# GNN layer, one core: a new order of work at the entry to the joint loop, and of the marks in the last three steps

## What is computed

```python
h = jnp.maximum(_layernorm(x, axis=-1), 0.0)
rel_inputs    = concatenate([h[senders], h[receivers], relations], axis=-1)
rel_effects   = relu(rel_inputs @ re_w1 + re_b1) @ re_w2 + re_b2
agg_effects   = segment_sum(rel_effects, receivers, num_segments=50000)
effect_inputs = concatenate([h, agg_effects], axis=-1)
out = x + relu(effect_inputs @ ea_w1 + ea_b1) @ ea_w2 + ea_b2
```

## Time and profile before

| | |
|---|---|
| median of 3 runs | 955.74 us (954.33 to 956.46) |
| the profiled execution, its own time | 956.01 us |
| its span | 954.1 us |
| PE busy | 923.3 us, 97% of the span |
| PE weight loads | 817.8 us, 86% |
| DVE busy | 740.1 us, 78% |
| ACT busy | 605.5 us, 63% |
| POOL busy | 609.1 us, 64% |

### The profile page before, as it was taken

The page is one execution under the profiler, slowest core; times in us unless marked ns, Lnnn a source line. Parts: engine busy times, 40 slices in busy tenths (PEclk is TensorE's granted clock), DMA queues, the critical chain, the costliest instruction groups (busy, mean ns, idle before and its releaser), DMA issues.

```text
span 954.1 us, 21049 instructions
## 1 busy us (share of the span) xinstructions
PE 923.3 (97%) x6450; PEld 817.8 (86%) x6450; DVE 740.1 (78%) x2155; ACT 605.5 (63%) x1180; POOL 609.1 (64%) x600
## 2 busy tenths in 40 slices
PE   4879999999999999999999999999999999999987
PEld 4668998898898899889889889988988988998876
DVE  5887788788788878878877887886887788788562
ACT  1447666666666766666666676666666667666653
POOL 7785776776677677677667767767766776772320
PEclk7979999999999999999999999999999999999999
DMA  6253655555565565555556556555555655554442
GB/s 200 75 148 113 183 163 168 150 177 175 151 186 168 151 183 163 168 151 176 172 155 185 167 153 183 162 169 158 169 174 151 186 167 152 169 177 146 124 123 76
DMA packets 114105, 151.88 MB, mean 159 GB/s; under 512 B 17984, under 2 KB 70080, under 8 KB 113984
## 3 DMA queue, kind: packets, MB, share of 16 engines
q1 hardware_dynamic: 101440, 124.73, 43.2%
q0 software_dynamic: 12544, 25.72, 10.2%
HBM read 104.92 MB, written 45.46 MB: 158 GB/s over the span
## 4 chain that ended last, share of the span: by engine, by line
PE 94%; DVE 3%; SPq 1%; issue 1%; ACT 1%; DMA 0%; DVEq 0%
PE l_ps L531 33%; PE l_ps L546 27%; PE l_ps L536 17%; PE agg_ps L496 7%; PE edge_ps L479 4%; PE node_ps L487 4%; PE node_ps L471 1%; SPq L294 0%; DVE rel_row L831 0%; DVE hot L844 0%; SPq L300 0%; DVE lo L804 0%; DVE h L797 0%; DMA drow_i<-in_dst_rows 0%; DMA win<-rel_rows 0%
## 5 line engine op out<-in xcount | busy, mean ns | idle before, releaser
L386 POOL DMA_INDIRECT gath<-in_x,dst_all x196 | 200.2, 1022 | 59.7 <-issue 59.7
L386 POOL DMA_INDIRECT gath<-in_x,src_all x196 | 195.0, 995 | 52.9 <-issue 51.7
L546 PE MATMUL l_ps<-w2n,hid 128*128 128x128 f32 x1568 | 193.6, 277 | 0.0
L655 ACT ACTIVATE hid<-l_ps,b1n 128x512 f32<-128x512 f32 x196 | 135.0, 689 | 82.4 <-PE l_ps L536 82.4
L409 POOL TENSOR_TENSOR ea_lo<-ea_in,ea_hi 128x512 fp32r<-128x512 f32 x45 | 74.3, 1651 | 171.6 <-ACT ea_hi L629 171.6
L546 PEld LDWEIGHTS l_ps<-w2n,hid 128*128 128x128 f32 x1568 | 182.9, 192 | 0.1
L810 DVE SCALAR_TENSOR_TENSOR lo<-node_ps,hi 128x512 fp32r<-128x512 f32 x98 | 67.3, 687 | 146.1 <-ACT hi L638 146.1
L663 ACT ACTIVATE h<-xin,shift,rs 128x128 f32<-128x128 f32 x392 | 165.2, 486 | 0.0
L531 PE MATMUL l_ps<-hi,w1n_hi 128*128 128x512 f32 x392 | 155.7, 397 | 0.4 <-ACT hid L655 0.4
L531 PE MATMUL l_ps<-hi,w1n_lo 128*128 128x512 f32 x392 | 155.4, 396 | 0.0
L402 POOL TENSOR_TENSOR xb<-xin,b2n 128x512 f32<-128x512 f32 x98 | 131.0, 1354 | 33.5 <-DVE res L838 33.5
(11 more groups left out here) (98 smaller groups left out, 1566.1 us busy)
## 6 DMA issues: line engine op xcount, KB each, us to landing
win<-rel_rows SPq DMA_DIRECT2D x392, 98.0 KB
xin<-in_x_tiles SPq DMA_DIRECT2D x98, 256.0 KB, 4.2
out<-res SPq DMA_DIRECT2D x98, 256.0 KB, 3.4
rel_rows<-rel_row SPq DMA_DIRECT2D x49, 392.0 KB, 2.4
ea_in<-in_ea_t SPq DMA_DIRECT2D x49, 256.0 KB, 3.2
gath<-in_x,src_all POOLq DMA_INDIRECT x196, 2.7
gath<-in_x,dst_all POOLq DMA_INDIRECT x196, 2.9
w1e<-in_L_gnn_re_w SPq DMA_DIRECT2D x1, 384.0 KB, 3.6
```

What stands on the lines that cost most here:

```text
L386: nc.gpsimd.indirect_dma_start(gath[b][:, s, k, :], None, x, bass.IndirectOffsetOnAxis(ap=idx[:, e * T + k:e * T + k + 1], axis=0)).then_i ...
L546: last = nc.tensor.matmul(l2_ps[turn % 2][:, k * P:(k + 1) * P], hid[r][:, c, k * P:(k + 1) * P], w[:, c, :], start=(c == 0), stop=(c == C ...
L655: nc.scalar.activation(hid[r][:, c, :], l1_ps[c][:, :], ACT.Relu, bias=b[:, c:c + 1]).then_inc(hid_set, 1)
```

## The change

On POOL the copies of the destinations of groups 0 and 1 (`set_dst`) go behind the gathers of group 1 instead of one in each step, that of group 2 behind the gathers of group 4, and the first pair's two `keep_x` move from ahead of group 5's gathers to behind the lo part of group 4's edge features. For the first, DVE makes the float copy of the destinations (`dst_f`) right behind `compare_rows`.

On ACT the first pair's two `normalise` move from the end of edge step 2 to either side of its first `hidden`. On PE only the transposes of tile 1 of the first pair stay ahead of joint step 3; its sum, and tile 2's transposes and sum, go behind the first layer of edge group 3. ACT and DVE follow: in joint step 3 the first pair's sums are split after the edges' `hidden` on ACT and, on DVE, after the statistics of group 4 and pair 1.

In the three pair steps DVE does `mark` of the next tile 1 ahead of `prepare`, and `mark` of the next tile 2 ahead of tile 1's lo parts. Nothing else in the pair steps is changed, on no engine.

```diff
@@ POOL
+            set_dst(0)
+            set_dst(1)
             def edge_step(e, last, fast):
-                set_dst(e)
                 if e + 2 < EG:
                     gather(e + 2)
-                if last:
+                if e > 1:
+                    set_dst(e)
+                if last and not fast:
                     pool.wait_ge(loaded[1], LOADS)
                     for r in (1, 2):
                         keep_x(r, 0, fast)
@@ POOL, joint_step
                     low_ea(e + 1)
+                if j == 0:
+                    pool.wait_ge(loaded[1], LOADS)
+                    for r in (1, 2):
+                        keep_x(r, 0, True)
@@ PE
+                if last and fast:
+                    turn_nodes(1, 0)
             def enter(fast):
...
-                for r in (1, 2):
-                    turn_nodes(r, 0)
-                    (sum_window if fast else sum_windows)(r, 0)
+                if not fast:
+                    for r in (1, 2):
+                        turn_nodes(r, 0)
+                        sum_windows(r, 0)
@@ PE, joint_step
                     for c in range(C):
                         layer1(r, n, turn + r, c)
+                    if r == 0 and j == 0:
+                        sum_window(1, 0)
+                        turn_nodes(2, 0)
+                        sum_window(2, 0)
@@ ACT, edge_step
+                if last:
+                    normalise(1, 0, True)
                 hidden(0, turn, 0, before_edge(e, fast))
+                if last:
+                    normalise(2, 0, True)
                 hidden(0, turn, 1, before_edge(e, fast))
...
-                if last:
-                    normalise(1, 0, True)
-                    normalise(2, 0, True)
@@ ACT, joint_step
+                if j == 0:
+                    hidden(0, turn, 0, before_edge(e, True))
+                    hidden(0, turn, 1, before_edge(e, True))
+                    high_sums(1, 0, True)
+                    high_nodes(2, 0, True)
+                    normalise(1, 1, True)
+                    deviations(e + 1, e + 1, pair_of(e + 1))
+                    normalise(2, 1, True)
@@ DVE
             compare_rows()
+            dve.wait_ge(idx_loaded, 32)
+            nc.vector.tensor_copy(dst_f[:, :], dst_all[:, :]).then_inc(dst_cast, 1)
             find_starts()
...
             def enter(fast):
...
+                if fast:
+                    low_features(1, 0)
+                    mark(1, 0)
+                    mark(2, 0)
@@ DVE, joint_step
                 spreads(*what)
+                if j == 0:
+                    low_sums(1, 0)
+                    low_nodes(2, 0)
@@ DVE, pair_step
                 more = j + 1 < NJ
+                if more and fast:
+                    mark(1, j + 1)
                 if j + 2 < NJ:
                     prepare(stats_turn(j + 2, fast), None, j + 2)
                 if j > 0:
                     node_results(2, j - 1, fast)
+                if more and fast:
+                    mark(2, j + 1)
                 if more:
-                    (mark if fast else mark_all)(1, j + 1)
+                    if not fast:
+                        mark_all(1, j + 1)
                     low_nodes(1, j + 1)
```

More of the change, by code:

```diff
@@ L634, in high_edges, with high_features, high_sums, high_nodes @@
                     nc.scalar.activation(hi[0][:, q, :], edge_ps[q][:, :], ACT.Relu).then_inc(edge_hi_set, 1)
-            def high_nodes(r, j, fast):
+            def high_features(r, j):
                 act.wait_ge(nodes_turned, tile_no(r, j) + 1)
                 nc.scalar.activation(hi[r][:, 0, :], node_ps[:, :], ACT.Relu).then_inc(node_hi_set, 1)
+            def high_sums(r, j, fast):
                 act.wait_ge(win_used[r], (j + 1) * (1 if fast else WINDOWS))
                 nc.scalar.activation(hi[r][:, 1, :], agg_ps[:, :], ACT.Copy).then_inc(agg_hi_set, 1)
+            def high_nodes(r, j, fast):
+                high_features(r, j)
+                high_sums(r, j, fast)
             def edge_highs(e, fast):
@@ L692, in edge_step @@
                 edge_mids(e)
-                if last:
-                    normalise(1, 0, True)
-                    normalise(2, 0, True)
             def enter(fast):
                 act.wait_ge(loaded[1], LOADS)
-                for r in (1, 2):
-                    high_nodes(r, 0, fast)
+                if fast:
+                    high_features(1, 0)
+                else:
+                    for r in (1, 2):
+                        high_nodes(r, 0, fast)
             def joint_step(e, j):
@@ L704, in joint_step @@
                 more = j + 1 < NJ
-                if more:
-                    normalise(1, j + 1, True)
-                hidden(0, turn, 0, before_edge(e, True))
-                if more:
-                    normalise(2, j + 1, True, range(0, 2))
-                deviations(e + 1, some(e + 1, EG), pair_of(e + 1))
-                hidden(0, turn, 1, before_edge(e, True))
-                if more:
-                    normalise(2, j + 1, True, range(2, T))
+                if j == 0:
[6 more added lines that the diff above has]
+                    normalise(2, 1, True)
+                else:
+                    if more:
+                        normalise(1, j + 1, True)
+                    hidden(0, turn, 0, before_edge(e, True))
+                    if more:
+                        normalise(2, j + 1, True, range(0, 2))
+                    deviations(e + 1, some(e + 1, EG), pair_of(e + 1))
+                    hidden(0, turn, 1, before_edge(e, True))
+                    if more:
+                        normalise(2, j + 1, True, range(2, T))
                 hidden(1, turn + 1, 0, before_node(1, j, True))
@@ L928, in _ @@
             low_edges(0)
-            dve.wait_ge(idx_loaded, 32)
-            nc.vector.tensor_copy(dst_f[:, :], dst_all[:, :]).then_inc(dst_cast, 1)
             split_weights(1)
@@ L952, in enter @@
             def enter(fast):
-                for r in (1, 2):
-                    (mark if fast else mark_all)(r, 0)
-                    low_nodes(r, 0)
+                if fast:
+                    low_features(1, 0)
+                    mark(1, 0)
+                    mark(2, 0)
+                else:
+                    for r in (1, 2):
+                        mark_all(r, 0)
+                        low_nodes(r, 0)
             def joint_step(e, j):
@@ L993, in pair_step @@
                 if more:
-                    (mark if fast else mark_all)(2, j + 1)
+                    if not fast:
+                        mark_all(2, j + 1)
                     low_nodes(2, j + 1)
```

## The result

| | before | changed |
|---|---|---|
| median of 4 runs each | 955.92 us (954.33 to 956.46) | 961.29 us (961.14 to 964.17) |
| the profiled execution, its own time | 956.01 us | 961.24 us |
| its span | 954.1 us | 959.4 us |
| PE busy | 923.3 us | 922.4 us |

The account below looks back on a forecast made before the run. PE was taken as the bound, so only its waits in head and tail could change: -4.2 + 6.6 = +2.4 us, giving 958.1 us against the median 955.74. The range was 954.4 to 960.8 us.

Parts of the forecast that it names:

- The tail's mechanism: Pair step 46: DVE's `mark` waits for windows, delaying `prepare`, `sd`, `hidden`; PE idles 7.7 us, then runs at half clock.
- The first rival: Tail: PE keeps 2.4 GHz after its long idle; tail costs 4.4, head gains 4.4, time 955.7 us; chance 0.15.
- The second rival: Tail: the wait is taken up and only the head counts; 950.5 to 951.5 us, or up to 954; chance 0.12.
- The head gains 3.9 to 4.4; I take 4.2.: Head, to the end of the first joint step's first layers: they end between 74.4 and 74.9, against 78.83.
- the statistics start at 61.65: Head, DVE: `rel_row` from 59.24, then one lo and two marks, 4 x 0.6 us; statistics start at 61.65, not 68.53.
- My low end for the head, 2.1: Head: if half clock lasted through tile 2's first layer also, the gain would be 2.1 us or so.
- my own range for the forecast: Whole time: 956.8 to 959.7 us, from head 4.4 with tail 5.5 to head 3.9 with tail 7.8.
- "I take 6.6" for the tail: Tail: pair step 48 starts 6.8 us late, taken as 6.6 because windows 2 may land up to 0.4 sooner.
- The third rival: First joint step: POOL's row of five operations holds DVE's `mark`, PE's sum 4.3 us late, 962.4 us; chance 0.08.

Follow-up runs that it names:

- experiments 3 and 5: 3: changed kernel with tile 2's `mark` back in its old place, 960.77 us; 5: changed kernel with ACT's `sd` behind all four `hidden`, 955.62 us.
- experiment 6: Changed kernel with unused filler matmuls on PE between the two first layers of pair step 46: 963.98 us with 60, 959.50 us with 30.
- experiment 2: Kernel before with only the change to DVE's pair steps, the head as before: 966.64 us, ratio 1.0104.
- experiment 1: Changed kernel with DVE's pair steps put back to the order of before, the new head kept: 953.79 us, ratio 0.9978.
- experiment 4: Changed kernel with tile 1's `mark` back behind `prepare`, tile 2's `mark` still ahead of tile 1's lo parts: 954.58 us, ratio 0.9987.
- experiment 8: experiment 1 plus, in joint step 3, DVE's tile 1 sums and tile 2 features between the statistics' halves and ACT's `hidden` and `ea_hi` earlier: 957.31 us.
- experiment 7: experiment 1 with POOL's two `keep_x` for the first pair back in edge step 2: 954.69 us, ratio 0.9989.
- experiment 9: experiment 8 with POOL's first two `xb` ahead of group 4's low halves, those behind DVE's `mark` of pair 1, ACT's `sd` one `hidden` earlier: 949.33 us.

## Why the prediction was wrong in size

**The tail's mechanism: right.** Measured from each execution's own head, PE's restart was forecast at 922.55 - 2.29 = 920.26 and came at 920.21. That it hangs on `prepare`, `sd`, `hidden` was shown by experiments 3 and 5. The first rival (the clock stays full) fell: the clock was 0.50 there, and experiment 6 prices it at 1.8 us. I had 2.3 for it (5.1 - 2.8), and the 12 matmuls took 4.65 us and not 5.1; in experiments 2 and 3 they took 5.14 and 5.28, so the size was fair and 4.65 is one case. The second rival (the wait is taken up) fell with the 6.46 us wait for windows.

**The step that failed first: "The head gains 3.9 to 4.4; I take 4.2."** It measured 2.3 in the profiled execution. Between the medians of experiment 1 and before it is also 2.3, but with some of it lost to the tail's clock. The sum in my working said that the statistics start at 61.65, behind `rel_row`, one lo and two marks in a row. It priced the marks as work and not as waits. In the trace of before tile 2's `mark` ran at 64.98, long after its windows were there, so no wait of DVE's showed when they land. Moved forward by 3 us, `mark` meets that landing. The old head ended at 78.66, and at 78.89 in experiment 2. Seven profiled executions have the new one (SP's two numbers are start and length of its row):

| execution | SP's row of eight loads | tile 2's `mark` | its wait | first layers end | difference |
|---|---|---|---|---|---|
| head alone (1) | 51.20, 6.77 | 60.15 | 0.56 | 74.27 | 14.12 |
| 30 fillers (6) | 51.54, 7.57 | 61.16 | 1.25 | 75.28 | 14.12 |
| 60 fillers (6) | 51.84, 7.66 | 61.55 | 0.92 | 75.67 | 14.12 |
| tile 2's mark early (4) | 52.16, 7.66 | 61.63 | 1.10 | 75.76 | 14.13 |
| tile 1's mark first (3) | 52.32, 7.94 | 62.23 | 1.63 | 76.42 | 14.19 |
| the changed kernel | 52.65, 7.83 | 62.24 | 0.58 | 76.37 | 14.13 |
| `sd` last (5) | 51.73, 6.73 | 60.45 | 0 | 74.05 | 13.60 |

In six of them the end of the head is tile 2's `mark` plus 14.1 us, and this `mark` waited for its windows. In the seventh it did not wait, and the second sum ran at full clock (0.85 instead of 1.44). My working had this `mark` at 61.05, so with the rows' 14.1 it would have given 75.2, a gain of 3.5. The other 0.7 of the first 1.9 us is for the most part the half clock that the second sum itself has, where I let it begin with tile 1's first layer: the seventh execution, with a sum at full clock, is 0.5 shorter. The remaining 1.2 are the `mark`, at 62.24 instead of 61.05. Of these, DVE's wait is 0.58, and the rest is that `rel_row`, ahead of it, also came 0.54 later in this execution (59.78 instead of 59.24). An earlier `rel_row` would have made DVE's wait longer by as much, since SP's last load, which it waits for, was issued by 60.48 in any case.

The landing could have been estimated before the run. In all seven the `mark` comes 1.8 to 2.2 us behind the end of the last of SP's eight issues. The trace of before has such a distance too: in its tail, SP's row at 915.01 ends after 6.62 us, and the `mark` that waits for it starts at 923.33, 1.7 us later. SP's row of before in the head (52.34, 6.74 us) ends at 59.08, which puts the landing at 60.8 to 61.3, beside the 61.05 of my working. The two short rows of SP in the table, 6.77 and 6.73, go with the two largest gains, 4.4 and 4.6. So 4.2 was within reach of this head. In the other five executions one of SP's eight issues took about 1 us more, and the row itself started between 51.54 and 52.65. What makes that issue long is open, and no run tests it. My low end for the head, 2.1, covered the measured size, but by another cause (half clock through tile 2), and I gave it little weight: my own range for the forecast took 3.9 as its low end.

**The second: "I take 6.6" for the tail.** It measured 7.7. The windows of tile 2 of pair 48 came 5.71 us behind tile 1's (935.38 to 941.09), and I had carried over 4.67 from the pair before. That is 1.0 of the 1.1 missing. The shorter half clock gave back 0.45. Of the other 0.5, 0.2 are what I had taken off for windows that might land sooner. Another 0.2 is that I measured the delay against the 940.37 of the chain, where the timeline has pair step 48 from 940.13.

**The third rival** was put down with 0.08 and missed by 0.20 us of distance on the trace. Experiment 8 moved POOL's row by 3 us and had the collision, but not on the `mark` that I named: on the `h` ahead of it. The Trainium skill's GPSIMD Engine Reference (Specifications) names both kinds, instructions with two SBUF inputs and those in a 2-port mode, and the Trainium skill's VectorE: DVE Perf Modes (Mode 2×_2P) counts a TENSOR_SCALAR in fp32 from SBUF to SBUF among the latter. The traces agree: `h` 6.97 us instead of 2.14, 2.94 instead of 1.11. I had quoted only the half of the sentence that fitted the row I had.

**What stays open.** When an idle time of 2 to 3 us on PE has half clock behind it. 2.39 us left the clock full in two executions (before, experiment 9) and not in a third (experiment 1). 2.51 left it full (60 fillers), 2.54 and 2.62 did not (30 fillers, experiment 4). 3.01 left it full in the changed kernel and not in experiment 2. 7.6 us had half clock behind them in all three cases. The price was 1.6 us in experiment 1 and 2.8 in experiment 2. Open is also why one of SP's issues is long in some executions.

## What to carry to other kernels

When an instruction is moved ahead, what it waits for must be priced at its new place. Where nothing waited for a transfer, the trace of before has no wait to show when it landed, so take its issue from the queue's row and add the time that other rows show from issue to landing. A wait moved to the front of an in-order engine costs what stands behind it on that engine and on the next ones, so follow the results of the instructions behind it to the first engine that has no work; here one `sd` behind 2.4 us of statistics made 6.5 us of waiting for windows into 7.6 on PE. And work that is moved on GpSimd has to be checked against what VectorE does at that time, instruction by instruction: the changed kernel missed a collision by 0.2 us, and experiment 8 lost 5 us to one. Last, one profiled execution is one case: the same head ended at 74.05 and at 76.42.

## What the runs showed of the hardware that I had not expected

- Beside POOL's row of five, DVE got one `h` through for each of POOL's operations (five of 1.30 us). Beside a row of two, one DVE instruction was held through what was left of both: `h` 2.18 us (experiment 7), `rel_row` 2.35 (before), `total` 1.98 (experiment 9). What decides between the two is not shown. POOL is hardly slowed (its `ea_lo` 1.36 us in experiment 8, 1.27 with DVE elsewhere). Where DVE's `hot` was first by 0.2 us, it kept its 0.68, and POOL's `ea_lo` took 1.63.
- Not every DVE instruction is hit: the eight statistics at 64.41 in experiment 9, of one SBUF input each, took the same 1.64 us as elsewhere, with `xb` running from 65.46.
- A small instruction is hit like a large one: `total`, 32 elements a partition, 1.98 us against 0.20.
- Idle times of PE of 2.4 to 3 us are sometimes followed by half clock (four times) and sometimes not (four times), at the same place of nearly the same program.
- An fp32 matmul of the fillers appears as two records of 0.113 us (13.56 us for 120).
- SyncE's queue needs 6.62 us for eight window loads whose starts it reads between them, and 4.55 with the starts read ahead.
